# Transposing the second weight block of each group on the tensor engine, with four queues reordered around it

## The reference

```
x = x + layernorm(attention(layernorm(x)))
x = x + layernorm(ffn(layernorm(x)))

ffn(x):  h = x @ (tern(w_fc) * scale).T + gate * (x @ v.T @ fast_b.T @ u.T)
         r = max(h, 0)
         return (r*r) @ (tern(w_proj) * scale).T
scale = clip(mean(|w|, per row), 1e-5);  tern(w) = clip(round(w / scale), -1, 1)
```

## Time and profile before

| what | value |
|---|---|
| time, median of 3 runs | 1076.35 us (1075.03 to 1078.9) |
| the profiled execution's own time | 1073.45 us |
| span of its slowest core (core 2) | 1071.9 us |
| spans of the other cores | 1067.5 to 1071.8 us |
| PE busy, share of the span | 94% |
| DVE, ACT, POOL busy | 53%, 34%, 5% |
| DMA, mean share of 16 engines | 45% over the span, near 100% from 60 to 225 us |

### The profile page before, as it was taken

How to read it: one execution, slowest core, us unless ns; L and a number is a source line. 1 busy time by engine, 2 the same in 40 slices (tenths; PEclk the granted TensorE clock), 3 DMA queues, 4 the chain that set the end, 5 groups by cost and what they waited for, 6 DMA issues and landing times.

```text
span 1071.9 us, 14984 instructions; the slowest of 8 cores (1067.5 to 1071.9 us)
## 1 busy us (share of the span) xinstructions
PE 1007.4 (94%) x4933; PEld 455.6 (43%) x4933; DVE 562.9 (53%) x813; ACT 361.5 (34%) x697; POOL 48.6 (5%) x105
## 2 busy tenths in 40 slices
PE   3688969999999999999999999999999999999997
PEld 1233334444444444444444444445444444444443
DVE  3679878745654545453445445633445353544333
ACT  4678788530003431143212341124301332013200
POOL 1111121000001000000000000000000000000000
PEclk9999889999999999999999999999999999999999
DMA  8699999942564125710455124622145401411021
GB/s 271 167 247 257 208 241 203 205 104 79 152 163 109 55 50 113 163 48 8 75 136 109 50 36 95 141 63 62 47 111 138 79 21 30 118 50 40 1 66 53
DMA packets 106367, 116.93 MB, mean 109 GB/s; under 512 B 82333, under 2 KB 82589, under 8 KB 106292
## 3 DMA queue, kind: packets, MB, share of 16 engines
q1 hardware_dynamic: 102324, 103.64, 38.7%
q0 software_dynamic: 3728, 12.25, 6.2%
q10 hardware_dynamic: 240, 0.07, 0.0%
HBM read 87.79 MB, written 17.31 MB: 98 GB/s over the span
## 4 chain that ended last, share of the span: by engine, by line
PE 82%; DVE 5%; issue 4%; DMA 4%; ACT 2%; POOL 1%; SPq 1%; ACTq 0%; DVEq 0%; POOLq 0%
PE pjp L649 38%; PE fcb L632 31%; PE pjp L632 2%; PE xp L799 1%; PE xp L649 1%; PE xp L762 1%; PE fcb L649 1%; DVE below L1443 1%; ACT rpp L1030 1%; PE pt L632 1%; DMA r<-v 1%; DMA Sfc<-tern 1%; ACT absd L1070 1%; PE pjp L696 1%; POOL rthr L521 1%
## 5 line engine op out<-in xcount | busy, mean ns | idle before, releaser
L632 PE MATMUL fcb<-xnT,Sfc 128*128 128x512 bf16 x1792 | 410.0, 386 | 8.1 <-DVE r L1425 4.9
L649 PE MATMUL pjp<-Spj,r 128*128 128x512 fp8e4 x1664 | 365.1, 379 | 1.7 <-DVE r2b L1425 1.7
L632 PEld LDWEIGHTS fcb<-xnT,Sfc 128*128 128x128 bf16 x1792 | 172.0, 99 | 229.0 <-issue 39.1
L1425 DVE TENSOR_TENSOR r<-fcb,rpp 128x512 bf16<-128x512 f32 x192 | 131.3, 690 | 224.7 <-ACT rpp L1030 224.5
L649 PEld LDWEIGHTS pjp<-Spj,r 128*128 128x128 bf16 x1664 | 160.5, 98 | 194.5 <-issue 5.0
L1030 ACT ACTIVATE rpp<-fcb,hsc 128x512 f32<-128x512 f32 x192 | 130.4, 686 | 208.5 <-PE fcb L632 199.3
L993 ACT ACTIVATE lv<-mv,cvecs 128x1 f32<-128x1 f32 x64 | 18.7, 293 | 281.2 <-DVE mv L1370 204.8
L1360 DVE TENSOR_TENSOR xy<-pjp,oscb 128x512 f32<-128x512 f32 x60 | 41.3, 689 | 130.2 <-PE pjp L649 130.2
L649 PE MATMUL pjp<-Spj,r2b 128*128 128x512 fp8e4 x256 | 55.4, 379 | 0.0
L1365 DVE BATCH_NORM_STATS2 s<-xy 128x6 f32<-128x512 f32 x64 | 44.4, 694 | 9.4 <-DVE xy L1360 6.0
L632 PE MATMUL pjp<-xnT,Sfc 128*128 128x512 bf16 x176 | 42.0, 390 | 6.2 <-ACT rpp L1030 4.7
(11 more groups left out here) (181 smaller groups left out, 704.8 us busy)
## 6 DMA issues: line engine op xcount, KB each, us to landing
xy<-x SPq DMA_DIRECT2D x31, 512.0 KB, 4.4
out<-xy SPq DMA_DIRECT2D x31, 512.0 KB, 3.0
xs<-x SPq DMA_DIRECT2D x25, 512.0 KB, 4.6
xy<-wfc SPq DMA_DIRECT2D x16, 512.0 KB, 5.8
xy<-wpj SPq DMA_DIRECT2D x16, 512.0 KB, 5.9
stg<-wfc SPq DMA_DIRECT2D x10, 512.0 KB, 6.0
stg<-wpj SPq DMA_DIRECT2D x8, 512.0 KB, 4.9
xs<-wpj SPq DMA_DIRECT2D x8, 512.0 KB, 5.4
```

The lines of the kernel that those rows point to most:

```text
L632: mm = te.matmul(bank, s_fc[:, dci * HF + hc * 128:dci * HF + hc * 128 + 128], xnT[:, dci * TT:(dci + 1) * TT], start=(dci == 0), stop=(dc ...
L649: mm = te.matmul(dst, squares(j)[:, hc * TT + s * 128: hc * TT + s * 128 + 128], spj_even[:, hc // 2, hc % 2, half * 512:half * 512 + 512] ...
L1425: ve.tensor_tensor(squares(j)[:, hc * TT:(hc + 1) * TT], bank, rpp[n % 2][:], ALU.mult).then_inc(v_r2, 1)
```

## The change

Four edits, in the 64 steps alone.

1. `BY_PE` is 1, 5, 9, ..., 29 and 31 instead of 3, 7, ..., 31: nine units by PE instead of eight, and in each group the second instead of the fourth.
2. PE: from step 4 on `ut` stands behind the step's `low_rank` and no longer ahead of it.
3. ACT: `evac` stands behind the step's sum and no longer ahead of it.
4. Tile 1's chunks 0 to 15 are spread over steps 35 to 47 instead of 37 to 47.

```diff
-BY_PE = [n for n in range(NFU) if n % 4 == 3]
+BY_PE = [n for n in range(NFU) if n % 4 == 1 or n == NFU - 1]
...
-    CHUNKS[37 + 11 * c // 16 if c < 16 else 17 + 2 * c if c < 20 else 36 + c
+    CHUNKS[35 + 13 * c // 16 if c < 16 else 17 + 2 * c if c < 20 else 36 + c
...
-                if n == 1 or (n > 1 and n % GRP == 0 and n + 4 < NFU):
-                    ut(n // GRP + 1)
+                if n == 1:
+                    ut(1)
                 if n + 3 < NFU:
                     low_rank(n + 3)
+                if n > 1 and n % GRP == 0 and n + 4 < NFU:
+                    ut(n // GRP + 1)
...
-                if n in BY_PE:
-                    evac(n)
                 if n in STATS:
                     rstd1(STATS[n])
...
                 for u in SUMS[n]:
                     abssum(u)
+                if n in BY_PE:
+                    evac(n)
```

## The result

| | before | changed |
|---|---|---|
| median of the runs | 1077.2 us (4) | 1109.88 us (4) |
| range, without the two below | 1075.03 to 1078.9 | 1091.18 to 1094.08 |
| ratio to before | | 1.0144 [1.0118, 1.017] |
| profiled execution, its own time | 1073.45 us | 1094.08 us |
| spans of the cores | 1067.5 to 1071.9 us | 1080.7 to 1092.5 us |

By it the changed kernel takes 1077.2 x 1.0144 = 1092.7 us. That is 15.5 us more than before, where 4.6 were forecast, and above the range's end of 1088.

The account below looks back on a forecast made before the run. DVE was taken as the bound in the w_fc groups, PE from T48 (first product with w_proj). Terms 3.4 - 2.9 + 5.0 - 2.5 + 0 - 0.3 + 1.7, plus 0.2, make +4.6: 1081.0 us, range 1071.5 to 1088.

Parts of the forecast that it names:

- I take two slow groups of four: Cuts 12 to 28: two of four groups have PE at half clock after its idle stretch; +5.0 us.
- the -2.5 before cut 12: Start to cut 12: unit 15's load comes earlier, so cut 12 is at 67.9 against 70.41; -2.5 us.
- the -0.3 for cut 28 to T48: Cut 28 to PE's first product with w_proj: unit 29 and early chunks together; -0.3 us, between -4.7 and +2.
- the wait: Four groups: cut 4G waits for ACT's copy of u's turn until stats1's start S + 8.37 us; +3.4 us.
- what it removes: Groups: low rank 4G-1 no longer waits for u, so DVE's waits of 1.21 and 1.69 are counted anew; -2.9 us.
- the clock: Groups: PE may run at half clock after idling around u's turn; +5.0 us, bounds nothing and 17.6.
- PE's start at T48: First product with w_proj: PE idles before it, so the first eight matmuls take 3.5 instead of 1.8; +1.7 us.
- the worse rival: Groups: PE's idle time is one piece and every group starts slow; +9.4 us, 1085.8, chance 0.22.
- Unit 29 off the DMA queue: Before cut 33: one DMA transpose less, so DVE's whole wait of 3.07 us goes.
- PE would turn tile 1 some 4 us earlier: Behind cut 28: PE gets through the turns of tile 1 some 4 us earlier, measured from cut 28.
- The chunks two steps earlier: Cuts 28 to 47: early gain lost again, cut 38 at 28.1 us behind cut 28 (27.5 before); -0.3 with unit 29.
- The sum ahead of `evac`: ACT in the four groups: its 2 us waits for PE go but were cover; 0, bounds 0 to -1 us.

Follow-up runs that it names:

- e4: Changed kernel with up to 13 unused PE matmuls right behind each turn of u, to keep PE busy; ratio 1.006.
- e1: Kernel before with edit 1 alone (units 1, 5, ... 29 and 31 by PE); ratio 1.0075.
- e5: Kernel before with edit 4 alone (tile 1's chunks spread over steps 35 to 47); ratio 1.0039.
- e7: Changed kernel with edit 4 undone, so the chunks are where they were; ratio 1.0091.
- e3: Changed kernel with the transposes of units 5 to 29 moved behind the step's low rank product; ratio 1.0062.
- e6: Kernel before with edit 3 alone (ACT's copy of a unit behind the step's sum); ratio 0.9995.
- e10: Changed kernel with edit 1 undone (units 3, 7, ... 31 by PE again); ratio 1.0004.
- e9: Kernel before with edit 4 and twenty unused PE matmuls ahead of PE's first product with w_proj; ratio 1.0035.
- e2: Kernel before with edit 2 alone (u's turn behind the step's low rank product); ratio 0.9966.
- e8: Kernel before with edit 2 and unused PE matmuls ahead of each turn of u; ratio 0.9947, median 1072.64 us.

## Why the prediction was wrong

Its direction was right, and so was its mechanism in the groups. The steps that failed are three terms of the sum: "I take two slow groups of four" (three were slow on every core), the -2.5 before cut 12 (+0.3), and the -0.3 for cut 28 to T48 (+3.7). In us, forecast against the difference of the two profiled executions (whose sum has 2 to 3 us of chance in it):

| step of the prediction | forecast | profiles |
|---|---|---|
| groups: the wait, what it removes, the clock | +3.4 - 2.9 + 5.0 | +9.1 |
| before cut 12 | -2.5 | +0.3 |
| cut 28 to T48 (unit 29, chunks) | -0.3 | +3.7 |
| PE's start at T48 | +1.7 | +2.3 |
| sum | +4.6 (0.2 unassigned) | +15.5 |

**The wait, right.** 0.76 to 0.78 us in place of 0.86 where the clock is full, and cut 4G at S + 8.36 where S + 8.37 was forecast. With the clock held (e4) the groups cost +1.3, forecast +0.5.

**The clock, the right mechanism and too few slow groups.** "I take two slow groups of four" failed. On every core one of the cuts 16, 20, 24, 28 waited the short 0.8 us; the other three waited 2.07 to 3.50, 2.88 on the mean, so 2.1 each more. With the 1.35 to 1.66 at six of the cuts behind (1.1 per core) that makes 7.5 us a core, about the 7.9 that e4 gives back. The price per slow group, 2.5 us, was right; their number was not. The step went wrong where it took the rate from the 14 rows with 2.06 to 2.66 us of idle time. In the new queue the idle time isn't broken by u's turn, as I had written myself under the worse rival: before L714 there are 24 stretches of 3.0 us or more on the 8 cores. I should have taken that class from the queue and not the one in the middle. The Trainium skill (TensorE: Matmul & The Clock Gate, HAM oscillation) says that a loop with such a gap pays at each turn; its example waits for DMA, in gaps mostly longer than these. The trace agrees in three groups of four. The prediction's rival with all four groups slow has 1085.8, nearer than the forecast but still low.

**Before cut 12, wrong in two ways.** The forecast had cut 12 at 67.9 where core 2's row says 70.41, and took the difference, -2.5, as the gain. But core 2 was late there: the mean of the 8 cores is 68.70, so 1.7 of the 2.5 were this core's row and not a gain. In the changed kernel the mean is 68.99. ACT's copy came when it was forecast (63.9 on the mean, 64.1 forecast), but from the copy to cut 12, forecast at 3.81 us, it took 3.8 on only two cores and 5.2 to 6.3 on the six where PE started slow, 5.1 on the mean. I had priced this stretch at full clock.

**Unit 29 off the DMA queue, right.** 28 to 33 is 1.8 us shorter, and the wait of 3.07 before cut 33 is at most 0.76. I counted a gain of 3.07 from core 2's row, which was the largest of the 8 (0.39 to 3.07). What was wrong is that PE would turn tile 1 some 4 us earlier, measured from cut 28: with edit 1 alone (e1) it does so 1.4 us earlier (17.24 against 18.63), in the changed kernel 1.9 later (20.51).

**The chunks two steps earlier, the largest miss.** I followed loads and sums and had cut 38 at 28.1 us behind cut 28, against 27.5 before. Measured on the mean: 32.1 against 26.8. e5 shows that edit 4 alone takes 4.6 of it, by DVE's wait at chunk 1's square. I had the dependency (relu of chunk 1 behind the sum of unit 43) and mis-sized it: the relu stands behind two sums and a whole relu and square of chunk 0, and a DVE that has caught up waits for all of these. The gain behind cut 38 (-2.3, forecast -0.9) doesn't repay that.

**The copy of unit 31, left out.** The other 2.5 of the +7.1 are in neither e5 nor e1, but e7 has 2.3 of them. PE of the changed kernel, core 7:

```profile
146.22 0.61 PE L714 MATMUL pt<-identb,tern 128*128 128x128 bf16 x8
...
153.13 2.42 PE L632 MATMUL fcb<-xnT,Sfc 128*128 128x512 bf16 x8 [2.78 <-ACT Sfc L1063]
155.34 1.91 PE L595 MATMUL pjp<-identb,xn 128*128 128x128 bf16 x16
```

and ACT of the same core:

```profile
148.41 1.04 ACT L1072 ACTIVATE absd<-xy 128x1024 fp8e4<-128x1024 f32 x1
...
149.45 0.67 ACT L1032 ACTIVATE rpp<-fcb,thr 128x512 f32<-128x512 f32 x1
...
150.93 1.06 ACT L1072 ACTIVATE absd<-xy 128x1024 fp8e4<-128x1024 f32 x1
...
151.99 1.00 ACT L1063 ACTIVATE Sfc<-pt 128x1024 bf16<-128x1024 bf16 x1
```

Unit 31 lies transposed in `pt` before 147 us, and its copy starts at 151.99, behind two sums and a relu and square; edit 3 put the last sum ahead of it. PE waits 2.78 us, turns tile 1 slowly, and DVE gets the turned rows at 158.11 after a wait of 2.87. "The sum ahead of `evac`" was put at 0, and argued for the groups only. The runs show that unit 31 is another case: in all six runs with edit 3 (changed, e3, e4, e6, e7, e10) PE waits for this copy, 0.9 to 4.3 us on 47 of 48 cores, and in none of the eight runs without it. In e6, with the edit alone and PE at full clock, DVE then waits 0.78 us on the mean for the turned rows (0.06 before), too little for the time to show. In e7 it waits 2.20. There PE was slow on two cores only, and on the six others DVE still waited 1.74 on the mean, as on core 1. PE, then DVE:

```profile
149.19 1.89 PE L632 MATMUL fcb<-xnT,Sfc 128*128 128x512 bf16 x8 [2.55 <-ACT Sfc L1063]
150.91 1.06 PE L595 MATMUL pjp<-identb,xn 128*128 128x128 bf16 x16
...
152.52 0.69 DVE L1391 COPY xnT<-pt 128x1024 bf16<-128x1024 bf16 x1 [2.16 <-PE pt L595]
```

So in e7 most of it is the copy and 0.5 us the slow clock. In the changed kernel PE was slow there on five cores: 3.17 us on these and 1.13 on the other three make 2.40, about half of it the clock's.

**PE's start at T48, right.** The idle time is 3.41 to 5.46 us and the first eight matmuls take 2.93 to 3.57 us. The forecast stopped at these eight; the next ones are slow in part too (2.51 in the row at 190.82 of e5), so it is 1.6 to 2.9 us and not 1.7. e9 shows the cause.

**The sum of the parts.** By the mean spans e1, e2, e5 and e6 make +6.9 - 3.0 + 4.2 - 0.3, about +7.7, the change +13.4. Most of the missing 5.7 comes in when edit 1 meets 2 and 3: e7 is at +8.4 where its three parts make +3.6. Of that, e2's gain of 3.0 is lost in the groups behind the new wait (61.93 and 61.92), and unit 31's copy comes later in e7 than in e6. Edit 4 on top of these costs 5.0, alone 4.2. The prediction added its terms as if they stood alone.

## What to carry to other kernels

Before a unit of work is moved, ask what stands between the copy that everybody waits for and the instruction that the bounding engine waits for: here eight small transposes and a tile product there made DVE wait 0.8 us per group at full clock and 2.1 to 3.5 at half clock, while with the transposes behind the low rank product the groups were back within 0.6 us of before (e3). Count PE's idle time in the new queue as one piece from the last instruction before it to the first behind it, and price what follows on the path at half clock. Take the base of such a term from the mean of the cores: two of the gains here, before cuts 12 and 33, came from the rows of one late core. Work moved ahead on an engine that is about to wait is no gain: the chunks' squares made DVE wait for ACT with a cut queued behind them.

## What the runs showed of the hardware

The same idle time before the same transposes was followed by either clock. In the changed kernel, of 24 stretches of 3.00 to 3.52 us before L714 17 were followed by slow work and 7 were not, as the 3.03 at 132.41 shows; of the 10 with 2 to 3 us 9 were. At T48, in the changed kernel, e3, e4, e5 and e10, idle times of 3.41 to 5.70 us were followed by a slow start on all 40 cores, and those of 0.68 to 1.86 us in the kernel before on none of its 8. There is no sharp border between these lengths: before u's turn in the kernel before, 5 of the 8 idle times of 1.60 to 1.89 us were followed by slow work too.

Matmuls that nobody reads keep the clock: up to 13 of them in 3 us of each group (e4) and up to 8 (e8) held it at 1.00 on 8 of 8 cores.

The two profiled executions alone would have misled on the spread: before's cores lie 4.4 us apart in its profile, the changed kernel's 11.8, but over all runs it is 10.4 to 11.0 (before) and 11.1. Where a group starts slow by core and run, one profile is one draw.
